# Queries of two attentions go to their stacks within SBUF, VectorE makes the third attention's first keys, and the trees normalise five groups ahead of the late scales

## The reference

```python
x = x + L0_xattn(layernorm(x), ctx, ...)   # 16 heads of 8, masked by tokens
x = x + L0_ffn(layernorm(x), ...)          # six experts, rotation
x = x + L1_xattn(layernorm(x), ctx, 32)    # keeps the 32 largest scores
x = x + L1_ffn(layernorm(x), ...)          # 16 experts, one per token
x = x + L2_xattn(layernorm(x), ctx, ctx, mask2)   # "third attention"
x = x + L2_ffn(layernorm(x), ...)          # three trees give q, k, v of a self-attention
x = x + L3_xattn(layernorm(x), ctx, ctx, mask3)   # "fourth attention"
x = x + L3_ffn(layernorm(x), ...)          # int8 linear
```

## Time and profile before

| | |
|---|---|
| median of 3 runs | 1319.48 us (1318.56 to 1325.87) |
| the profiled execution, its own time | 1321.31 us |
| span, first to last instruction | 1319.5 us |
| mean granted TensorE clock | 0.854 |
| busy PE / DVE / ACT / POOL | 1029.1 / 862.7 / 581.3 / 465.1 us |
| third attention | about 685 to 848 us |
| trees | about 851 to 1132 us |
| fourth attention | about 1133 to 1260 us |

### The profile page before, as it was taken

One profiled execution on the slowest core, in us unless ns is written; L12 is line 12 of the kernel. 1 busy time (PEld: TensorE's weight loads), 2 busy tenths in 40 slices (PEclk: granted clock), 3 DMA queues, 4 the chain that ended last, 5 costly groups with the idle time before them and its releaser, 6 DMA issues. The chain is left out here.

```text
span 1319.5 us, 20756 instructions
## 1 busy us (share of the span) xinstructions
PE 1029.1 (78%) x6368; PEld 765.4 (58%) x6368; DVE 862.7 (65%) x2917; ACT 581.3 (44%) x1169; POOL 465.1 (35%) x593
## 2 busy tenths in 40 slices
PE   4688879899999965763962788588999999488832
PEld 1565648788888854333751556365677677256522
DVE  7667873767888795995227777565444446357778
ACT  2466445445656653310322565312344355357521
POOL 0434300122222232703728444107730755334221
PEclk9789979999999975557895699759999999689965
DMA  8234134000000004041423433003267831143202
GB/s 284 81 107 120 47 98 126 1 1 2 9 10 9 9 11 127 0 128 31 110 61 99 119 106 77 4 1 99 76 202 203 231 82 39 58 128 98 70 1 64
DMA packets 112561, 103.18 MB, mean 78 GB/s; under 512 B 11008, under 2 KB 92288, under 8 KB 112064
## 3 DMA queue, kind: packets, MB, share of 16 engines
q1 hardware_dynamic: 80704, 76.31, 20.5%
q0 software_dynamic: 6400, 12.92, 3.7%
q10 hardware_dynamic: 25344, 12.59, 3.3%
HBM read 64.23 MB, written 37.75 MB: 77 GB/s over the span
## 5 line engine op out<-in xcount | busy, mean ns | idle before, releaser
L861 DVE TENSOR_REDUCE mha_nm<-mha_pS 128x16 f32<-128x1024 f32 x96 | 117.1, 1220 | 24.5 <-PE mha_pS L623 24.4
L801 POOL TENSOR_TENSOR mha_ks<-KS,w_ctx 104x1024 fp32r<-104x1024 f32 (+1 forms) x48 | 90.9, 1895 | 96.8 <-POOLq L100 53.3
L1328 ACT ACTIVATE ffn_hid<-ffn_pH,w_ffn 128x512 f32<-128x512 f32 x128 | 85.0, 686 | 45.9 <-PE ffn_pH L1116 44.4
L744 ACT ACTIVATE XH<-mha_pST 128x1024 f32<-128x1024 f32 x96 | 97.8, 1019 | 11.3 <-PE mha_pST L644 11.1
L623 PE MATMUL mha_pS<-mha_ks,mha_qs 96*128 96x256 f32 (+1 forms) x384 | 80.9, 338 | 23.7 <-DVE mha_nm L861 19.0
L1129 PEld LDWEIGHTS ffn_pE<-W2R,ffn_hid 128*128 128x128 f32 x768 | 93.6, 192 | 4.5
L1129 PE MATMUL ffn_pE<-W2R,ffn_hid 128*128 128x128 f32 x768 | 94.0, 276 | 0.0
L1599 DVE SCALAR_TENSOR_TENSOR ffn_acc<-ffn_pE,ffn_wt,ffn_acc 128x128 f32<-128x128 f32 x192 | 53.8, 343 | 55.5 <-PE ffn_pE L1129 54.1
L623 PEld LDWEIGHTS mha_pS<-mha_ks,mha_qs 96*128 96x128 f32 (+1 forms) x384 | 59.4, 214 | 40.5 <-issue 21.4
L2575 POOL DMA_INDIRECT leaf_rows<-XH,tree_place x64 | 62.8, 981 | 55.9 <-DVE tree_place L2655 36.6
L2670 DVE SCALAR_TENSOR_TENSOR tree_hl<-tree_pH,tree_hh 128x512 fp32r<-128x512 f32 x64 | 43.9, 687 | 39.0 <-ACT tree_hh L2481 36.0
(11 more groups left out here) (560 smaller groups left out, 2782.5 us busy)
## 6 DMA issues: line engine op xcount, KB each, us to landing
mha_qs<-queries SPq DMA_DIRECT2D x72, 256.0 KB, 4.1
tree_leaf<-in_leaves_dram SPq DMA_DIRECT2D x96, 96.5 KB
queries<-mha_qh SPq DMA_DIRECT2D x24, 256.0 KB, 2.1
queries<-mha_ql SPq DMA_DIRECT2D x24, 256.0 KB, 2.5
leaf_rows<-ffn_none SPq DMA_DIRECT2D x12, 512.0 KB, 6.4
tree_xs<-leaf_rows ACTq DMA_DIRECT2D x24, 256.0 KB, 3.4
leaf_results<-tree_ys ACTq DMA_DIRECT2D x24, 256.0 KB, 3.9
EW<-in_L_W_dram SPq DMA_DIRECT2D x32, 128.0 KB, 2.7
```

What stands on the lines that cost most here:

```text
L744: act.activation(PT[b % PB][:, CU * i:CU * i + CU, :], pST[:], ACT.Exp, scale=SC).then_inc(s["P"], 1)
L801: pool.tensor_tensor(ks[b % KB][0:K1, :, :, :], kb, hb, ALU.mult).then_inc(s["k"], 1)
L861: dve.tensor_reduce(nm[:, t, :], pS[:], AX.X, ALU.max, negate=True).then_inc(s["nm"], 1)
L1328: act.activation(hid[p % 2][:, c, :], pH[c][:], ACT.Gelu, bias=b).then_inc(s["h"], 1)
```

## The change

Three parts. (1) In the third and fourth attention (`direct`), `qh` and `ql` get two buffers, and SP moves their rows straight into the stack: for each of the three copies and each of the four head groups one DMA of 32 rows x 512 fp32, twelve a quad. The first three quads are issued in the slot of the old writes, the later ones in the slot of the old reads. ScalarE waits, before it overwrites a `qh` buffer, until the twelve DMAs of the quad before last have landed. (2) In the third attention VectorE makes the keys of batches 0 to 3 ahead of its first `arrive`; GpSimd gathers without a break. (3) In the trees VectorE normalises five groups, then takes the late scales, then the last three groups, the splits and the memsets; ScalarE evacuates three groups before the root.

```diff
-        qh, ql = st.sb("qh", [P, QS], F32R), st.sb("ql", [P, QS], F32R)
+        direct = not key_mask
+        QW = 2 if direct else 1
+        qh, ql = ([st.sb(f"{n}{u}", [P, QS], F32R) for u in range(QW)] for n in ("qh", "ql"))
...
-        LD, LM, LW = 16 * 3, 16, 16 * 2
+        LD, LM, LW = 16 * (3 * NQ if direct else 3), 16, 16 * 2
...
+            def spread_queries(q):
+                u = q % QB
+                sp.wait_ge(s["q"], q + 1)
+                need(sp, s["ST"], QT * (q - QB) + QT)
+                for n, src in enumerate((qh, qh, ql)):
+                    for g in range(NQ):
+                        sp.dma_start(plain(qs[u][HR * n:HR * n + HR, g, :]), plain(src[q % 2][HR * g:HR * g + HR, :])).then_inc(s_ld[u], 16)
...
                 if t % QT == 3 and live(t + 5):
-                    write_queries(quad(t + 5))
+                    if not direct:
+                        write_queries(quad(t + 5))
+                    elif quad(t + 5) < QB:
+                        spread_queries(quad(t + 5))
...
                 if t % QT == 2 and live(t + 2):
-                    read_queries(quad(t + 2))
+                    if not direct:
+                        read_queries(quad(t + 2))
+                    elif quad(t + 2) >= QB:
+                        spread_queries(quad(t + 2))
...
-                need(act, s["qw"], LW * q)
-                act.activation(qh[:], pQ[:], ACT.Identity, bias=w("bq")).then_inc(s["qh"], 1)
+                if not direct:
+                    need(act, s["qw"], LW * q)
+                elif q >= QW:
+                    act.wait_ge(s_ld[(q - QW) % QB], LD * ((q - QW) // QB + 1))
+                act.activation(qh[q % QW][:], pQ[:], ACT.Identity, bias=w("bq")).then_inc(s["qh"], 1)
...
             if gather:
-                gathers(0)
-                gathers(1)
-                keys(0)
-                keys(1)
-                gathers(2)
-                gathers(3)
-                keys(2)
-                keys(3)
-                for q in range(4, NG):
+                for q in range(NG):
                     gathers(q)
-                keys(KB)
+                keys(pool, KB)
...
             dve.memset(pO[:], 0.0).then_inc(s["zero"], 1)
             if gather:
+                for b in range(KB):
+                    keys(dve, b)
                 arrive(0)
...
-            x_evac(0)
+            for g in range(3):
+                x_evac(g)
             rs_act(act)
-            for g in range(1, NG):
+            for g in range(3, NG):
                 x_evac(g)
...
+            for g in range(NG - 3):
+                normalise(g)
+            rs_dve(dve)
+            for g in range(NG - 3, NG):
+                normalise(g)
+            split(0)
+            split(1)
             for u in range(2):
                 ins = dve.memset(hid[u][LW:LW + 1, :], 1.0)
             ins.then_inc(s["ones"], 1)
-            normalise(0)
-            rs_dve(dve)
-            for g in range(1, NG):
-                normalise(g)
-            split(0)
-            split(1)
```

More of the change, by code:

```diff
@@ L550, in split_shift, with keys @@
             eng.tensor_tensor(nx[b % 2][:, :, :, 1, :], src, nx[b % 2][:, :, :, 0, :], ALU.subtract).then_inc(s["nx"], 1)
+        def keys(eng, b):
+            need(eng, s["ST"], TB * (b - KB) + 2)
+            kb = KS[0:K1, :, SK * b:SK * b + SK].unsqueeze(2).to_broadcast([K1, NQ, NH, SK])
+            hb = heads[0:K1, :].unsqueeze(1).unsqueeze(3).to_broadcast([K1, NQ, NH, SK])
+            eng.tensor_tensor(ks[b % KB][0:K1, :, :, :], kb, hb, ALU.mult).then_inc(s["k"], 1)
         @blk.sync
@@ L557, in write_queries @@
                 sp.wait_ge(s["q"], q + 1)
-                for n, src in enumerate((qh, ql)):
+                for n, src in enumerate((qh[0], ql[0])):
                     sp.dma_start(core.qd[n, q], plain(src[:])).then_inc(s["qw"], 16)
@@ L795, in gathers @@
                                             bounds_check=N1 * CAP - 1, oob_is_err=False).then_inc(s_g[q % 4], 16)
[L797 to L801, removed]
             def add_bo(b):
@@ L822, in _ @@
                 for b in range(KB):
-                    keys(b)
+                    keys(pool, b)
                     if key_mask and b < QB:
@@ L831, in _ @@
                 if 2 <= b < B - 2:
-                    keys(b + 2)
+                    keys(pool, b + 2)
                 if gather:
@@ L850, in q_low @@
                     dve.wait_ge(s["qh"], q + 1)
-                    dve.scalar_tensor_tensor(ql[:], pQ[:], w("bq"), qh[:], ALU.add, ALU.subtract).then_inc(s["q"], 1)
+                    dve.scalar_tensor_tensor(ql[q % QW][:], pQ[:], w("bq"), qh[q % QW][:], ALU.add, ALU.subtract).then_inc(s["q"], 1)
                 def largest(t):
```

## The result

The changed kernel is slower: 1346.98 us (median; 1343.69 to 1351.30) against 1320.24 us (1318.56 to 1325.87) of the kernel before on the same chip, four runs of each; ratio 1.0197, 95% interval 1.0169 to 1.0225. The prediction was 1309.4 us. The profiled execution took 1343.69 us, with a span of 1341.8.

A forecast was written before the change was run, and what follows sets the result against it. No engine is full throughout; at stage starts one chain from engine to engine sets the time. Gains of 5.9 (third attention), 0.3 (fourth) and 3.9 (trees) sum to 10.1 us, giving 1309.4 us; range 1303.5 to 1316.5.

The forecast's parts named there:

- c: SP's issue time for a quad's twelve SBUF-to-SBUF transfers: 0.37 us each, 4.4 us in all, bounds 3.7 to 5.0.
- rival C: Dear pieces on SP make both attentions late: break-even at 0.55 us a piece, 1339 us at 0.67; chance 0.05.
- First scores of the fourth attention: Fourth attention's start: SP's first piece to first scores takes 6.1 us instead of 8.69, a gain of 2.6.
- Slot 3: Pieces between shifts write and read-back take 6.4 us: third attention loses about 0.3 us, fourth 2.3.
- Steady quads: From quad 3 on, pieces need 6.1 us against 8.06 available, so cost and gain are none.
- the table load: Third attention, slot 3: ScalarE's table load hides most of a 1.9 us lateness; about 0.3 us remains.
- Its formula: Total gain near 28.4 - 4c; above c = 6.36 each of ten steady quads also waits c - 6.36.
- The 5.9 us forecast for the third attention: Third attention: gain of 6.2 us at the first maximum, less about 0.3 in slot 3; bounds 3.9 and 6.5.
- Rival A: Third attention's start: VectorE's key products hold the gathers up to 4.9 us; total gain 5.2, 1314.3 us; chance 0.12.
- what was to be late next: Trees: ScalarE's root comes at 858.5, yet group 5 is normalised by 861, before TensorE wants it at 863.9; hidden.

The follow-up runs named there:

- parts 1 and 3: Changed kernel with the queries sent through DRAM again, keys on VectorE and the new trees' order kept: 1315.60 us, ratio 0.9961 to the kernel before.
- part 1 alone: Kernel before with only the third attention's first keys moved to VectorE, queries through DRAM and trees as before: 1320.27 us, ratio 1.0001.

## Why the prediction was wrong

**The step that failed** is in part 2: "I take 0.37 between them ... twelve take c = 4.4 us (bounds 3.7 to 5.0)". It measured 0.63 and 7.5. Both bounds came from rows with one end in DRAM, and I took them for bounds of a transfer that has none. The text said under rival C that no row prices an issue from SBUF to SBUF, but gave this unknown a far end of only 5.0 us and let everything behind it rest on that. The argument "32 rows less than 128" also fell: 16 rows or 32, 1 KB or 2 KB a row, the price was the same. The estimate from the Trainium skill ("SBUF — State Buffer", "The DMA setup-cost knee"), 0.475 us by a rate in bytes, was nearer, but the price is not a rate either.

**What hung on c.** First scores of the fourth attention: 6.1 us forecast, 9.84 measured (7.5 + 0.8 for one long issue + 1.5 to the landing). Slot 3: 6.4 forecast, 9.66. Steady quads: I compared 6.1 with 8.06 and called the cost none; it is 9.75 from 768.66 to 778.41, and the wait 1.61. In the third attention, slot 3 takes 9.63 us (728.25 to 737.88), 5.1 more than before, and costs 2.9: the table load hides some 2 us, as forecast. The path was right in each case, the term c wrong in each.

**Rival C is what happened**, at a chance of 0.05. Its formula at c = 7.5 gives 28.4 - 30 - 10 x 1.14 = -13 us. (It is 0.7 too high: at c = 4.4 it gives 10.8, where the sum is 10.1.) The medians differ by -26.7; the two profiled executions, from which the table above comes, by 1319.5 - 1341.8 = -22.3 (the changed kernel's was the fastest of its four). Against these, term by term: the third attention's start and slot 3 give 2.6 - 2.9 = -0.3 (formula 15.3 - 15 = 0.3), the fourth's -1.2 - 6.2 = -7.3 (formula -5.9), the trees 3.65 (3.9), the ten steady steps -19.2 (formula -11.4), and the steps to quad 1, which it lacks, 0.5. So most of what the formula misses is in the steady steps. I left two things out there: the granted clock that falls to 0.50 behind a wait, and the shifts write that SP does only after the burst (777.03). How the 7.8 us divide between the two was not separated.

**Part 1.** The 5.9 us forecast for the third attention are for parts 1 and 2 together; of the 6.2 at its first maximum the text gave part 2 about 3, which leaves some 3 for part 1. Alone it is worth 0.0 us, within 2.8. The four products took 1.15 us each (forecast 1.2), and the long 128x4 operations are gone: right. Two things were wrong. Rival A holds for two gathers: the first arrival was at 694.21 and not at 692.2, the second group's sum at 699.55 and not at 697.4. And the gain was reckoned against one execution in which the pair had caught `ve`. Against that one, parts 1 and 3 bring the first maximum 2.65 us sooner (34.63 to 31.98), near the forecast. In another execution of the same kernel it comes 2.4 us sooner by itself, and there part 1 brings 0.3 or, with the 32.28 of part 1 alone, nothing. Which of them was profiled was chance. On the rule that decides rival A, the Trainium skill, "SBUF — State Buffer", "Who interferes with whom", infers that a VectorE operation on two tensors leaves descriptor work of GpSimd alone, as it takes only the shared read side. Here the gathers were stretched: 1.84 and 1.97 us beside the keys, 1.00 with the keys on ScalarE. As a gather takes its row numbers from SBUF (`slots`), it may count as an instruction that reads SBUF, as the prediction left open; no run tells this from descriptor work.

**Part 3**, forecast 3.9 (3.4 to 4.5): 3.65 in the profile, and alone 0.31% (0.10 to 0.53), 4.1 us. Right. TensorE turns group 1 right behind group 0 (1.54 us later), and what was to be late next is not.

**The sum.** 10.1 us of gain were forecast. In its place: some 5 us of gain from parts 1 and 3, and 31.4 us of loss from part 2.

## What to carry to other kernels

Count the DMA issues of an in-order queue before the bytes: replacing two writes and three reads by twelve transfers took the DRAM round trip away and added 5.5 us of issue time per quad to a queue that also carries something urgent. A price that no row shows needs bounds from both sides of what could be different, and the conclusion has to survive the far one; here it held only to 0.55 us a piece. And where a stall depends on which of two short operations is caught, take a second profile of the same kernel before pricing its removal.

## What the runs showed of the hardware

- In a burst an issue from SBUF to SBUF takes SP 0.63 us, whether it moves 16 rows or 32, 1 KB or 2 KB a row; from DRAM to the same 32 rows 0.46 us. On ScalarE's queue it takes 0.67 to 0.72 us, at the same time.
- A shifts write right behind such a burst takes 0.59 us instead of 0.31, a shifts read 0.53 (1176.30) instead of 0.27. So part of what a piece costs may fall on the issue behind it; this was not separated.
- A wait of TensorE of 1.61 us at the end of a stretch at a granted clock of 0.98 was followed by 10 us at 0.50.
- VectorE's four key products of two SBUF tensors, back to back, stretched two gathers that GpSimd issued beside them from 1.00 to 1.84 and 1.97 us; the single sum of 0.73 us did not stretch the gather beside it.
- GpSimd's product held VectorE operations of 128x4 within SBUF, with two tensors (`nt`, 4.46 us) and with a single one (`ve`, 4.03 us). It did not hold the maximum, which reads PSUM (1.22 us, 25 times beside a product in the two attentions of the kernel before and 39 times not), nor the statistics of one tile of `X` (0.28 us).
